# Graph attention on one core: the fold of a chunk in spaced steps, and TensorE as the one that frees a group of counts

## The chip, the cores and the metric

The kernel runs on one core of a Trainium2 chip. The metric is the time of one execution on the device, in microseconds (us); lower is better. Within the core, TensorE (PE) multiplies matrices, VectorE (DVE) works elementwise, ScalarE (ACT) applies functions and copies, SyncE (SP) issues the loads. PEld is TensorE's loading of weights.

## The reference

Four residual graph layers over 6250 nodes with 64 features and 200,000 edges. Each one normalises x by rows, takes the positive part, and adds a graph operation of the result to x. The first is a degree-scaled sum over edges, the last a message-passing pair. Between them stand three attention passes over the same edges (and a loop at each node): the second residual layer has two of them one behind the other (64 to 32 features, then 32 to 64), the third has one (64 to 64). Each of the three has this form:

```
h = x @ W
logit(edge) = leaky_relu(h[src] @ a_s + h[dst] @ a_d, 0.2)
e = exp(logit - max over the edges of dst)
out[dst] = sum(e * h[src]) / sum(e) + b
```

## The kernel before

The edges are first counted into a dense matrix of 6272 x 6272 counts (49 x 49 blocks of 128), which lies in DRAM. Each attention layer l (0, 1, 2) then goes through it in 7 chunks of 896 target nodes (CW, 7 blocks). A chunk has 49 tiles r, one for each block of 128 source nodes: a tile is counts of 128 sources by 896 targets in fp16. Seven tiles are a group. SP loads groups into four buffers (CS = 4), each group in two transfers (`load_group`, line 668), and waits for `cnt_free` before it overwrites a buffer.

The leaky ReLU has two slopes, so the exponential of a logit splits into a product of a source factor and a target factor on either side of zero. For each tile:

- ACT writes the sign, 0 or 1, of (source score + target score) for each pair (`signs`, line 3366), into one of 7 places (RING).
- DVE multiplies it with the counts: `above` (`count_above`, line 2000; in layer 0, one tile of seven finds its sign by itself, line 1997). Then `below` = counts - above (`count_below`, line 2010). Layer 2 has a `below` for every tile. Layer 1 has none for tiles 0 and 2 of a group (the `whole` tiles), where PE takes the counts themselves and subtracts by a third set of matmuls (line 2751). Layer 0 has one for tiles 1 and 5 of a group only. `below` of tile r stands behind `above` of tile r + 1 on DVE.
- PE multiplies the blocks of both sides with weighted features and adds into PSUM (line 2740): 7 matmuls a side. The last three tiles of a chunk (LATE) are taken bank group by bank group (line 2772), so that ACT can copy the first banks out while PE still works on the others. `tile_used` tells ACT that the place of a tile is free; so ACT is at most 7 tiles ahead of PE.

At tile 4 (EVICT_AT) of the next chunk ACT copies the banks of the last one to SBUF (`keep_banks`, lines 3381 and 3383), before it makes the sign of tile 4. From tile 8 (FOLD_AT) DVE folds them: the three bf16 pieces of a sum are added and both sides are scaled by target factors and added, in 5, 9 and 4 steps (FOLD_STEPS; `fold_pieces` in layers 0 and 2, `fold_levels` in layer 1), one step behind each tile, at tiles 8, 9, 10 and so on. In the last chunk of a layer all steps stand together at tile 8.

In layer 1 the fold's last step gives means. PE turns them (`turn_means`, before tile TURN_AT = 17, line 2789), ACT keeps them (KEEP_AT = 24, lines 3390 and 3391), PE multiplies them with the layer's weights (`mix_means`, MIX_AT = 26, line 2800) and ACT writes the chunk's sums (`means_out`, OUT_AT = 33, line 3398). In layer 1's last chunk DVE also does the residual and the variance of finished chunks, in three parts behind tiles 13, 22 and 36 (`residual_early_split`; its k is the tile less 13).

In layer 0, PE frees a group of counts with its last matmul on it. In layers 1 and 2, DVE frees it, behind `below` of the group's last tile, with a drain (line 2012).

Of the kernel before, what the change touches and what calls it, by code (L numbers as in the profile page):

```python
# [69 lines left out]
LATE = 3  # L70
FOLD_AT = 8
FOLD_STEPS = (5, 9, 4)
TURN_AT = 17
KEEP_AT = 24
MIX_AT = 26
OUT_AT = 33
WHOLE = (0, 2)
LW = 3 * (D + 1)
UNITS = 4
# [22 lines left out]
def gnn_kernel(nc, ap, out):  # L102
    ctx = ExitStack()
    with ctx:
# [420 lines left out]
        def groups_full(l):  # L525

            return len(parts[l][7]) - (l > 0)
# [485 lines left out]
        def _(dve):  # L1013
# [592 lines left out]

            def residual_early_split(k):

                for i, (first, b0, b1) in enumerate(((0, 0, 16), (9, 16, 32), (23, 32, EARLY))):
                    if k == 0 and i == 0:  # L1610
                        si_columns(2)
                    if k == first:
                        dve.wait_ge(sums_kept, (3, 5, 6)[i])
                    for q, step in enumerate((mixed_bias, residual, mean_of, centred, squared, variance)):
                        if k == first + 1 + q:
                            step(b0, b1)
                if k == 31:
                    dve.sem_inc(root_in, 1)

            def residual_early(k, n=1):  # L1620
# [262 lines left out]
            def split_attention(l, n):  # L1883
# [118 lines left out]
                def count_below(c, r):  # L2002

                    g, j = divmod(r, GRP)
                    if whole(l, r):
                        return
                    if l == 1 and j == GRP - 1:
                        dve.wait_ge(tile_used, c * NB + (n * ROWS + g * GRP + max(WHOLE) + 1))
                    dve.wait_ge(above_ready, c * NB + (n * ROWS + r + 1))
                    nc.vector.tensor_tensor(below_at[r % RING], counts_of(g, j), above_at[r % RING], ALU.subtract).then_inc(below_ready, 1)  # L2010
                    if l > 0 and j == GRP - 1:
                        dve.drain().then_inc(cnt_free, 1)  # L2012

                def fold_pieces(c, k):

# [84 lines left out]
                def chunk(c, first, last):  # L2100

                    for r in range(NB):
# [7 lines left out]
                        if last and r == FOLD_AT:  # L2110
                            for k in range(FOLD_STEPS[l]):
                                fold(c - 1, k)
                        elif not first and not last and 0 <= r - FOLD_AT < FOLD_STEPS[l]:
                            fold(c - 1, r - FOLD_AT)
                        if last and r >= EARLY_AT:
                            if l == 0:
                                hidden_early(r - EARLY_AT, True)
# [161 lines left out]
        def _(pe):  # L2279
# [361 lines left out]
            def split_attention(l, n):  # L2641
# [72 lines left out]
                def tile(c, r, first):  # L2714
# [5 lines left out]
                    for side in range(2):  # L2720
# [13 lines left out]
                        for b in range(CB):  # L2734
# [6 lines left out]
                                                    start=(r == 0 and at == 0), stop=False, skip_group_check=True)  # L2741
                            if l == 0 and side == 1 and b == (CB - 1 if with_below(l, r) else 0):
                                last.then_inc(tile_used, 1)
                            if l == 0 and side == 1 and b == CB - 1 and j == GRP - 1:
                                last.then_inc(cnt_free, 1)
                    if whole(l, r):
                        if first and r == 0:
# [8 lines left out]
                def late_tiles(c):  # L2756

                    for k in range(len(groups)):
                        for r in range(NB - LATE, NB):
# [8 lines left out]
                            for i, (side, b) in enumerate(members):  # L2768
                                of = above_at[r % RING] if side == 0 else below_at[r % RING] if lower else counts_of(g, j)
                                bank, at = places[side][b]  # L2770
                                wide = wide3 if l == 0 and lower else moves[side].shape[2]
                                last = nc.tensor.matmul(psum[:, bank, at:at + wide], of[:, b * BLK:(b + 1) * BLK], moves[side][:, r, 0:wide],  # L2772
                                                        start=False, stop=(r == NB - 1), skip_group_check=True)
                                if k == len(groups) - 1 and i == (len(members) - 1 if lower else 0):
                                    last.then_inc(tile_used, 1)
                            if r == NB - 1 and k < groups_full(l):
                                last.then_inc(banks_full, 1)
                    if l == 0:
# [695 lines left out]
```

## Time and profile before

| what | value |
|---|---|
| median of 3 runs | 2841.45 us (2840.66 to 2842.64) |
| the profiled execution | 2841.15 us |
| its span (first to last instruction) | 2838.9 us |
| PE busy | 2431.0 us (86%) |
| DVE busy | 2203.5 us (78%) |
| ACT busy | 1548.5 us (55%) |
| the attention layers with what lies between them | 1034 to 2335 us |
| mean granted clock of TensorE | 0.942 |

Busy shares are means over stages with different limits; the attention layers are read chunk by chunk. The granted clock is a share of full speed: 1.00 is 2.4 GHz and 0.50 is 1.2 GHz. The durations of DVE's and ACT's instructions overlap in the records: a tile operation of DVE is recorded with 0.62 us, but the next one starts 0.535 us after it; a sign on ACT is recorded with 1.04 us and the next starts 0.935 us after it. So costs are taken from start to start.

### The profile page before, as it was taken

The page shows a single profiled execution, that of the slowest core. Times are in us where ns is not written, and L with a number is a line of the kernel's source. Part 1 is how long each engine was busy: PE and PEld are TensorE (multiplying, and loading weights), DVE is VectorE, ACT ScalarE, POOL GpSimd, SP SyncE. Part 2 cuts the span into 40 slices and gives each one's busy share as a digit, 9 for nine tenths or more (in the row PEclk, how much of TensorE's full clock was granted, in tenths as well). Part 3 has the DMA queues.
Part 4 walks back from the last instruction along what each step waited for, and adds up shares of the span by engine and source line. Part 5 has one row for each costly group of instructions (what it writes and reads, how often), then busy time and mean ns, then how long its engine had stood idle before and what let it go on. Part 6 is the DMA issues. An engine that isn't in the chain of part 4 may idle for free. (4 is left out here: it accounts for less than half of the span.)

```text
span 2838.9 us, 86445 instructions
## 1 busy us (share of the span) xinstructions
PE 2431.0 (86%) x31023; PEld 2188.3 (77%) x31024; DVE 2203.5 (78%) x4979; ACT 1548.5 (55%) x1943; POOL 424.0 (15%) x921
## 2 busy tenths in 40 slices
PE   2656999999999679999599998769999868999998
PEld 2644777677777569988599888669999858898997
DVE  8986899898899879999799899799999984222212
ACT  6004444444444289998799987588888740000101
POOL 1003555555556300000000000000000000000000
PEclk8877999999999889999899999989999979999999
DMA  3003443533435347676356655225655437888998
GB/s 107 0 0 87 127 127 88 166 87 108 145 87 149 99 160 266 234 265 215 104 189 205 226 181 181 91 92 183 204 181 181 158 115 247 308 306 299 330 366 299
DMA packets 398046, 494.28 MB, mean 174 GB/s; under 512 B 81925, under 2 KB 397289, under 8 KB 397674
## 3 DMA queue, kind: packets, MB, share of 16 engines
q1 hardware_dynamic: 364760, 487.44, 51.0%
q10 hardware_dynamic: 33044, 3.63, 1.0%
q8 instruction: 150, 2.46, 0.4%
q14 instruction: 92, 0.75, 0.1%
HBM read 401.81 MB, written 89.17 MB: 173 GB/s over the span
## 5 line engine op out<-in xcount | busy, mean ns | idle before, releaser
L2740 PE MATMUL psum<-sb_arena 128*128 128x99 bf16 (+2 forms) x13524 | 1011.3, 236 | 127.7 <-DVE sb_arena L2010 82.6
L2740 PEld LDWEIGHTS psum<-sb_arena 128*128 128x128 f16 x13524 | 969.7, 99 | 157.2 <-DVE sb_arena L2010 103.0
L3366 ACT ACTIVATE sb_arena<-sb_arena 128x896 f16 (+1 forms) x980 | 961.7, 1036 | 152.4 <-PE psum L2740 107.4
L2000 DVE TENSOR_TENSOR sb_arena<-sb_arena 128x896 f16<-128x896 f16 x980 | 593.0, 621 | 84.9 <-ACT sb_arena L3366 55.2
L3035 ACT ACTIVATE sb_arena<-psum 128x784 f16<-128x784 f32 x392 | 322.5, 823 | 394.6 <-PE psum L2385 226.5
L1280 DVE TENSOR_SCALAR sb_arena<-sb_arena 128x392 f16<-128x392 f16 x1960 | 486.9, 323 | 0.0
L2385 PE MATMUL psum<-sb_arena 64*128 64x392 f16 x3920 | 387.0, 341 | 70.1 <-ACT sb_arena L3035 25.0
L2835 PE MATMUL psum<-sb_arena 128*128 128x192 bf16 x4802 | 416.2, 248 | 30.4 <-DVEq L2157 15.2
L2835 PEld LDWEIGHTS psum<-sb_arena 128*128 128x128 f16 x4802 | 402.5, 98 | 46.0 <-DVEq L2157 16.1
L2010 DVE TENSOR_TENSOR sb_arena<-sb_arena 128x896 f16<-128x896 f16 x686 | 424.0, 618 | 0.3
L2385 PEld LDWEIGHTS psum<-sb_arena 64*128 64x128 bf16 x3920 | 258.3, 138 | 151.3 <-issue 79.8
L940 POOL TENSOR_TENSOR sb_arena<-sb_arena 128x15 f32<-128x15 f32 x392 | 252.4, 644 | 271.0 <-DVE sb_arena L1280 144.3
L2368 PE MATMUL psum<-sb_arena 128*128 128x195 bf16 x2940 | 286.8, 250 | 1.6 <-ACT sb_arena L3008 1.6
L2368 PEld LDWEIGHTS psum<-sb_arena 128*128 128x128 f16 x2940 | 241.6, 98 | 57.0 <-issue 54.1
L1277 DVE TENSOR_TENSOR sb_arena<-sb_arena 128x1280 bf16<-128x1280 bf16 x196 | 162.0, 827 | 76.3 <-PE psum L2385 56.5
L2310 PE MATMUL psum<-sb_arena 128*64 128x98 bf16 x1568 | 98.4, 228 | 61.5 <-DVE sb_arena L1140 61.3
L2310 PEld LDWEIGHTS psum<-sb_arena 128*64 128x64 bf16 x1568 | 90.0, 125 | 70.0 <-DVE sb_arena L1140 70.0
L1140 DVE TENSOR_TENSOR sb_arena<-sb_arena 128x2744 bf16<-128x2744 bf16 x112 | 141.1, 1334 | 3.2 <-PE psum L2310 2.0
L942 POOL CAST sb_arena<-sb_arena 128x5 bf16<-128x5 f32 x392 | 126.2, 322 | 0.0
L2255 DVE SCALAR_TENSOR_TENSOR sb_arena<-psum,sb_arena 128x256 f32<-128x256 f32 (+1 forms) x42 | 14.5, 386 | 141.9 <-PE psum L2835 140.8
L3442 ACT COPY sb_arena<-psum 128x896 f32<-128x896 f32 x7 | 6.3, 907 | 199.2 <-PE psum L2849 199.2
L3447 ACT ACTIVATE sb_arena<-sb_arena 128x448 f32<-128x448 f32 x7 | 4.0, 577 | 183.6 <-DVEq L2265 183.6
(381 smaller groups left out, 1444.5 us busy)
## 6 DMA issues: line engine op xcount, KB each, us to landing
sb_arena<-counts SPq DMA_DIRECT2D x245, 896.0 KB, 6.9
sb_arena<-counts SPq DMA_DIRECT2D x245, 672.0 KB, 4.6
counts<-sb_arena SPq DMA_DIRECT2D x56, 1344.0 KB, 6.7
sb_arena<-records SPq DMA_DIRECT2D x392, 5.0 KB, 2.1
sb_arena<-records ACTq DMA_DIRECT2D x392, 5.0 KB, 2.2
counts<-sb_arena SPq DMA_DIRECT2D x1, 5488.0 KB, 19.8
records<-sb_arena SPq DMA_DIRECT2D x1, 3124.0 KB, 8.9
counts<-sb_arena SPq DMA_DIRECT2D x14, 112.0 KB, 4.6
```

The source lines that it names most:

```text
L940: nc.gpsimd.tensor_tensor(rel[:, k % WH, :].rearrange("p (t c) -> p t c", c=3), both[:, :, 0:3], of.broadcast_to([BLK, ST, 3]), ALU.add)
L1277: nc.vector.tensor_tensor(sub_src[:, at // 2], iota_t[:, :, 0:2 * ST], src_rel[:, k:k + 2, :].rearrange("p w t -> p (w t)").unsqueeze(1).b ...
L1280: last = nc.vector.tensor_scalar(sub_key[:, at, t, :], sub_iota[:], rel[:, k, 3 * t:3 * t + 1], None, ALU.is_equal)
L2000: nc.vector.tensor_tensor(above_at[r % RING], above_at[r % RING], counts_of(g, j), ALU.mult).then_inc(above_ready, 1)
L2010: nc.vector.tensor_tensor(below_at[r % RING], counts_of(g, j), above_at[r % RING], ALU.subtract).then_inc(below_ready, 1)
L2310: last = nc.tensor.matmul(psum[0:M, 0, 0:W], hot_row[:, s, t // 2, :, t % 2], hot_col[:, s, t // 2, :, t % 2], start=False, stop=False, sk ...
L2368: last = nc.tensor.matmul(psum[p0:p0 + d1 - d0, 6 + u // 2, u % 2 * LW:(u % 2 + 1) * LW], stage[:, slot, r * HALF + d0:r * HALF + d1], LM[ ...
L2385: last = nc.tensor.matmul(banks_of(odd, k)[:, side, 0:NB * SUB], sub_src[rows, s // 2, :, k % 2 * ST + t], sub_key[rows, s, t, :], start=t ...
L2740: last = nc.tensor.matmul(psum[:, bank, at:at + wide], of[:, b * BLK:(b + 1) * BLK], moves[side][:, r, 0:wide], start=(r == 0 and at == 0) ...
L2835: last = nc.tensor.matmul(psum[:, bank + b % 4, at:at + 3 * D], counts_of(g, j)[:, b * BLK:(b + 1) * BLK], of[:, r, :], start=(r == 0 and ...
L3035: nc.scalar.activation(to[:, :, k // EG, :, k % EG, :].rearrange("p a k d -> p k a d"), banks_of(odd, k)[:, :, 0:NB * SUB].rearrange("p k ...
L3366: nc.scalar.activation(above_at[r % RING], of, ACT.Sigmoid, bias=steep_s[:, r:r + 1], scale=STEEP).then_inc(signs_ready, 1)
```

## The change

The steps of a middle chunk's fold stand 4, 2 and 8 tiles apart (FOLD_EVERY): layer 0 at tiles 8, 12, 16, 20, 24; layer 1 at 8, 10 and so on to 24; layer 2 at 8, 16, 24, 32. What stands behind the means in layer 1 moves back: turning from tile 17 to 27, keeping from 24 to 32, mixing from 26 to 34, the sums from 33 to 39. The third part of the residual in layer 1's last chunk starts at k = 28 instead of 23, and the root's signal comes at k = 35 instead of 31. In layers 1 and 2, a matmul of PE (the second block of the lower side of the group's last tile) frees the group of counts; DVE's drain with that signal is gone. DVE's wait for `tile_used` in layer 1 stays.

```diff
 FOLD_STEPS = (5, 9, 4)
-TURN_AT = 17
-KEEP_AT = 24
-MIX_AT = 26
-OUT_AT = 33
+FOLD_EVERY = (4, 2, 8)
+TURN_AT = 27
+KEEP_AT = 32
+MIX_AT = 34
+OUT_AT = 39
...
-                for i, (first, b0, b1) in enumerate(((0, 0, 16), (9, 16, 32), (23, 32, EARLY))):
+                for i, (first, b0, b1) in enumerate(((0, 0, 16), (9, 16, 32), (28, 32, EARLY))):
...
-                if k == 31:
+                if k == 35:
                     dve.sem_inc(root_in, 1)
...
                     nc.vector.tensor_tensor(below_at[r % RING], counts_of(g, j), above_at[r % RING], ALU.subtract).then_inc(below_ready, 1)
-                    if l > 0 and j == GRP - 1:
-                        dve.drain().then_inc(cnt_free, 1)
...
-                        elif not first and not last and 0 <= r - FOLD_AT < FOLD_STEPS[l]:
-                            fold(c - 1, r - FOLD_AT)
+                        elif not first and not last and r >= FOLD_AT and (r - FOLD_AT) % FOLD_EVERY[l] == 0 and (r - FOLD_AT) // FOLD_EVERY[l] < FOLD_STEPS[l]:
+                            fold(c - 1, (r - FOLD_AT) // FOLD_EVERY[l])
...
-                            if l == 0 and side == 1 and b == CB - 1 and j == GRP - 1:
+                            if side == 1 and b == (CB - 1 if l == 0 else 1) and j == GRP - 1:
                                 last.then_inc(cnt_free, 1)
...
                                     last.then_inc(tile_used, 1)
+                                if l > 0 and r == NB - 1 and (side, b) == (1, 1):
+                                    last.then_inc(cnt_free, 1)
```

## Rows read from the trace of the kernel before

**Rows 1.** Stretches (us): length, busy of PE, PEld, DVE, ACT, POOL, granted clock, DMA.

```profile
1168.00:1212.80 44.80, 41.80 (x687) 40.92 (x688) 41.48 (x69) 41.96 (x48) 0.00 (x0) 1.00 0.73 251
1400.80:1451.60 50.80, 50.80 (x784) 50.60 (x785) 48.56 (x88) 49.59 (x55) 0.00 (x0) 0.96 0.50 164
1563.50:1619.70 56.20, 52.70 (x796) 50.86 (x794) 51.49 (x102) 50.44 (x58) 0.00 (x0) 0.97 0.59 200
1571.50:1586.00 14.50, 11.00 (x141) 9.44 (x138) 12.77 (x31) 10.29 (x12) 0.00 (x0) 0.88 0.48 163
2050.70:2111.80 61.10, 58.64 (x689) 57.95 (x687) 57.21 (x104) 52.45 (x54) 0.00 (x0) 1.00 0.56 187
```

**Rows 2.** Waits from 1034 to 2335 us: total, times, longest.

```profile
PE psum L2740 <- DVE sb_arena L2010: 82.6, 72, 5.7
```

**Rows 3.** Timeline of DVE in layer 2, chunk 3: start, length, instructions, idle before.

```profile
2052.57 0.62 DVE L2000 TENSOR_TENSOR sb_arena<-sb_arena 128x896 f16<-128x896 f16 x1 [1.78 <-ACT sb_arena L3366]
...
2055.80 0.62 DVE L2000 TENSOR_TENSOR sb_arena<-sb_arena 128x896 f16<-128x896 f16 x1
...
2057.16 0.63 DVE L2000 TENSOR_TENSOR sb_arena<-sb_arena 128x896 f16<-128x896 f16 x1 [0.22 <-issue]
...
2066.11 0.63 DVE L2000 TENSOR_TENSOR sb_arena<-sb_arena 128x896 f16<-128x896 f16 x1 [0.19 <-issue]
...
2107.77 0.62 DVE L2010 TENSOR_TENSOR sb_arena<-sb_arena 128x896 f16<-128x896 f16 x1
```

**Rows 4.** Timeline of PE in the same chunk of layer 2.

```profile
2063.05 1.35 PE L2740 MATMUL psum<-sb_arena 128*128 128x195 bf16 x14 [0.90 <-DVE sb_arena L2010]
...
2067.33 7.88 PE L2740 MATMUL psum<-sb_arena 128*128 128x195 bf16 x91 [0.53 <-DVE sb_arena L2010]
...
2108.27 3.72 PE L2772 MATMUL psum<-sb_arena 128*128 128x195 bf16 x42
```

**Rows 5.** Timeline of DVE in layer 0, chunk 3.

```profile
1172.47 0.62 DVE L2000 TENSOR_TENSOR sb_arena<-sb_arena 128x896 f16<-128x896 f16 x1 [0.16 <-ACT sb_arena L3366]
...
1180.27 0.63 DVE L2000 TENSOR_TENSOR sb_arena<-sb_arena 128x896 f16<-128x896 f16 x1 [0.19 <-issue]
...
1191.50 0.62 DVE L2010 TENSOR_TENSOR sb_arena<-sb_arena 128x896 f16<-128x896 f16 x1
```

**Rows 6.** Timeline of PE in the same chunk of layer 0.

```profile
1181.49 15.75 PE L2740 MATMUL psum<-sb_arena 128*128 128x99 bf16 x262 [1.18 <-DVE sb_arena L2010]
```

**Rows 7.** Timeline of DVE in layer 1, chunk 3.

```profile
1569.73 0.63 DVE L2000 TENSOR_TENSOR sb_arena<-sb_arena 128x896 f16<-128x896 f16 x1 [0.21 <-issue]
...
1585.55 1.16 DVE L2000 TENSOR_TENSOR sb_arena<-sb_arena 128x896 f16<-128x896 f16 x2 [0.21 <-issue]
...
1595.50 0.61 DVE L2010 TENSOR_TENSOR sb_arena<-sb_arena 128x896 f16<-128x896 f16 x1
```

**Rows 8.** Timeline of PE in the same chunk of layer 1.

```profile
1586.66 0.67 PE L2789 MATMUL psum<-sb_ident,sb_arena 128*128 128x128 f32 x4
...
1596.01 1.01 PE L2800 MATMUL psum<-sb_W_att,sb_arena 128*128 128x264 f32 x4
1596.86 2.90 PE L2740 MATMUL psum<-sb_arena 128*128 128x198 bf16 x42
```

**Rows 9.** Timeline of ACT in the same chunk of layer 1.

```profile
1561.96 0.80 ACT L3383 COPY sb_arena<-psum 128x792 f32<-128x792 f32 x1
...
1564.06 12.24 ACT L3366 ACTIVATE sb_arena<-sb_arena 128x896 f16 x13
...
1597.30 0.51 ACT L3398 COPY sb_arena<-psum 128x448 f32 x1
1598.05 1.98 ACT L3366 ACTIVATE sb_arena<-sb_arena 128x896 f16 x2 [0.24 <-PE psum L2740]
```

**Rows 10.** Issues of DMAs: KB each, median us from issue to landing.

```profile
sb_arena<-counts SPq DMA_DIRECT2D x245, 896.0 KB, 6.9
```

**Rows 11.** Timeline of PE at the end of layer 1's last chunk.

```profile
1806.06 2.78 PE L2772 MATMUL psum<-sb_arena 128*128 128x198 bf16 x38 [0.56 <-DVE sb_arena L2010]
```

## The prediction

> **What bounds the kernel now.** I first read the stretches of the span chunk by chunk, taking one middle chunk of each attention layer [rows 1]. A middle chunk lasts 44.8 us in layer 0, 56.2 in layer 1 and 61.1 in layer 2. In each of them TensorE (PE), VectorE (DVE) and ScalarE (ACT) are all busy for over 85% of the time, so no single engine is the bound: the chain through the ring of seven tiles is. The list of waits shows where the loss appears: PE waits for `below` tiles of DVE 72 times, 82.6 us [rows 2].
>
> The timelines of one chunk then show who is late where. In what follows a chunk starts with PE's first matmul, at 1168.03, 1563.45 and 2050.71 us in the three layers. In layer 2, DVE has no free time after tile 4. It waits 1.78 us for the sign of tile 4, since ACT has just copied the banks, and after that it runs back to back to the next chunk [rows 3]. PE stands still only in the fold, at tiles 9 to 11: 0.90, two later waits of which the last is 0.53, then nothing [rows 4]. So a chunk is two chains joined at one tile: DVE from the sign of tile 4 to the tile where PE catches up, and PE from there to the end. The chunk's length is the largest value, over the tiles r, of "end of r's tiles on DVE, plus what PE has left from r". An edit pays only as far as it lowers this for every r.
>
> **What the change removes.** *The drain behind each group's last `below`* (layers 1 and 2, seven a chunk). Three tiles without it take 3.23 us on DVE (start of tile 4 at 2052.57 to start of tile 7 at 2055.80), 1.08 each; from tile 7 to tile 8, with it between, it is 1.36 (2055.80 to 2057.16) [rows 3]. So 0.29 us each, counting the exact 1.07 of two operations at 0.535. Its signal moves to a matmul that PE issues anyway; layer 0 has that form already, at no cost that I can see in its rows. Zero is the other bound for the drain, if DVE would have waited there anyway. The Trainium skill speaks for that zero (VectorE: DVE Perf Modes, Rules for kernel authors): a drain follows each DVE operation whatever one does, so count operations, not semaphores. By it the removal is worth nothing; the trace shows 0.29 us start to start for exactly this place, and I keep the row.
>
> *The fold's steps apart.* Their number and work stay the same. In layer 0, DVE goes from tile 8 at 1172.47 to tile 13 at 1180.27 [rows 5], 7.80 us; less five tile operations at 0.535 and the one of 1.07 (3.75), so 4.05 us of fold. In layer 1, tile 8 to 17 is 1569.73 to 1585.55 [rows 7], 15.82 us; 15 operations and one drain are 8.33, so the fold is 7.5. In layer 2, tile 8 to 12 is 2057.16 to 2066.11 [rows 3], 8.95 less 4 x 1.07 = 4.7. All this stays on DVE; spread, it only comes due later.
>
> **Layer 2, five middle chunks.** With steps at 8, 16, 24 and 32 and no drains, PE's stop at 9 to 11 goes. What ties next is the last tile: PE's late tiles begin at 2108.27 and touch tile 48 after eight matmuls of 0.085 us, at 2108.95 [rows 4]; DVE ends `below` of tile 48 at 2107.77 + 0.62 = 2108.39 [rows 3]. That is 0.56 us of slack, 0.50 after 0.06 for the signal, which is how far PE's starts stay behind DVE's ends in the fold. Six drains lie before it, 1.77 us. So the chunk shrinks by 2.27 to 58.8. PE's own floor is 686 matmuls x 0.0848 = 58.2. Tile 24, where three steps are done, gives 58.4 by the same sum, so tile 48 decides. I take 2.3 us x 5 = 11.5 us.
>
> **Layer 0, five middle chunks.** No drain is removed. All five steps are done by tile 24, so DVE ends `below` of tile 26 exactly as before: 1191.50 + 0.62 = 1192.12 [rows 5]. PE comes to it 196 matmuls after 1181.49 at 0.0594 us each, 1193.13 (15.5 us over 262 matmuls) [rows 6]: 1.0 us of slack, 0.95 with the signal. That is all the gain; before tile 26 the spread steps leave shorter sums (tile 22: 43.4 us). The chunk becomes 43.9; 0.9 x 5 = 4.5 us.
>
> **Layer 1, five middle chunks.** The steps end at tile 24, and turning the means (0.50 us on PE, 1586.66 to 1587.16) and mixing them (0.85, 1596.01 to 1596.86) [rows 8] now both come after tile 26 instead of before it. DVE ends `below` of tile 26 at 1595.50 + 0.61 = 1596.11 [rows 7], less three drains 1595.2. PE started the second side of tile 26 at 1596.86 + 7 x 0.085 = 1597.46, and needed 22.2 us to the chunk's end at 1619.7; now 22.2 + 0.50 + 0.85 = 23.6. Sum: 1595.2 + 0.06 - 1563.45 + 23.6 = 55.4 us. Second, ACT: `means_out` now stands 5 tiles behind the mixing, not 7, and the ring lets ACT be 7 ahead of PE, so ACT waits for the mixing at tile 39. PE is at tile 26's second side at 1595.27; the rest of it is 0.31 us, five plain tiles are 0.91 each (three take 2.74, from the row of 42 matmuls at 1596.86), two whole ones 1.21 [rows 8], 7.3 in all, so the mixing ends at 1595.27 + 7.3 + 1.35 = 1603.9; the copy costs ACT 0.75 (1597.30 to 1598.05); then sign 39 starts at 1604.7, 13 signs at 0.935 lead to sign 3 of the next chunk, and 0.935 and the bank copies (1561.96 to 1564.06, 2.10) to sign 4, at 1619.9: 55.8 after 1564.06 [rows 9]. Between 55.4 and 55.8 I take 55.6: 0.6 x 5 = 3.0 us.
>
> **The other chunks.** Chunk 0 has no fold and PE is bound in it (50.8 us, all of it PE busy, [rows 1]): nothing. The last chunks keep their fold in one piece at tile 8. In layer 1 DVE is bound to the end there (PE waits for it in the late tiles, [rows 11]), six drains at 0.25 (my estimate, a little under the 0.29 above, since some waiting is mixed in) give 1.5 us; the third part of the residual moves five tiles back but is the same work, and its wait for the sums is met by `means_out` at tile 39 against tile 41. In layer 2, DVE is bound up to tile 36: five drains, 1.3 us. After the layers nothing changes.
>
> **The loads.** PE frees a group of counts up to 3 us later than DVE did, in SP's queue. Tightest is group 2 of the next chunk: freed in the late tiles, about 1 us before the chunk starts, needed by DVE at tile 14, some 14 us into it. The larger half of a load lands 6.9 us after issue in the median [rows 10]; with group 3 queued beside it I bound it by twice that, 13.8. So even at that bound the 15 us cover it, by 1 us; a wait there would cost its own length once a chunk.
>
> **Sum.** 11.5 + 4.5 + 3.0 + 1.5 + 1.3 = 21.8 us. The profiled execution took 2841.15 us, 0.3 below the median of the three runs, so 2819.4 profiled and 2819.6 for the median.
>
> **The rivals.**
> *The forecast*, 2812 to 2827: 0.62.
> *Layer 1 gives nothing*, since the waits of ACT at tiles 32 and 39 eat it: 2822.6 to 2826. For it: DVE tile 48 of layer 1 would have only some 0.3 us left. 0.12.
> *All of PE's stops go*: PE busy is 41.8, 50.8 and 58.2 us a chunk, so 3.0 + 5.4 + 2.9 = 11.3, x 5 and 2.8: 2782. Against it: DVE's own work from tile 4 on, which spreading doesn't shorten. 0.07.
> *The drain is worth nothing*: then layer 2 gives 0.5 x 5, layer 0 4.5, layer 1 nothing: 7 us, 2834.4. This is the skill's rule above; the 0.29 us row speaks against it. 0.06.
> *Slower, by TensorE's clock.* Layer 1's fold stretch ran at a mean granted clock of 0.88, so partly at 1.2 GHz, after PE had idled in it; the chunk as a whole has 0.97 [rows 1]. After the change PE has many short waits over tiles 8 to 26 in place of a few long ones. If the low level held for that stretch, a layer-1 tile would cost PE about twice 0.91 us against DVE's 1.25 or so with the fold: 0.57 over 18 tiles is some 10 us a chunk, 50 in the layer: 2870. It decides from about 4 us a chunk on. Against it: the chunks of layers 0 and 2 ran at 1.00 all through, though PE idled some 2.5 us of the 6 from tile 9 to 12 in layer 2 [rows 1, 4]. The Trainium skill (TensorE: Matmul & The Clock Gate, Part 1) says that the throttled state is the default and activity lifts it; the trace agrees in layer 1 only, and sharper idling is what the change takes away. 0.06.
> *Late loads*: 2 to 3 us of waiting in each of ten chunks, 2840 to 2850; only if a load took over 15 us. 0.03. *No change*, from causes that I don't see: 0.04.
>
> **How the numbers follow.** 0.2% (5.7 us) is about what a measurement of this kernel tells from no change. Faster is the sum of the first four, 0.87; slower the clock and most of the late loads, 0.08; same 0.05. The range leaves out the clock, the full recovery and part of the drain's case: 2806 (layer 0 at its floor, layer 1 by its first sum, layer 2 at 58.2) to 2830.
>
> **What would show it.** Right: no drain row at the old place; middle chunks of 43.9, 55.6 and 58.8 us; PE's wait in one piece gone, short ones at tiles 12 to 26 in layers 0 and 1, and one at the late tiles of layer 2; ACT idle at tile 39 in layer 1. Wrong: DVE start to start still 1.36 across a group's end, DVE waiting for counts, or a clock under 1.00 in layers 0 and 2.

## The result, and the profile after

| | before | after |
|---|---|---|
| median | 2841.33 us (4 runs, 2840.66 to 2842.64) | 2821.56 us (4 runs, 2821.03 to 2825.98) |
| profiled execution | 2841.15 us, span 2838.9 us | 2821.03 us, span 2818.8 us |
| mean granted clock | 0.942 | 0.946 |

The ratio is 0.9933, with a 95% interval of 0.9921 to 0.9945: faster by 19.8 us, where 21.8 were forecast. In the kernel after, the line numbers differ from those of before by one: `above` is L2001, `below` L2011, the signs L3367, PE's tiles L2739 and its late tiles L2771.

The list of waits between 1034 and 2335 us, of the kernel after, in the columns of [rows 2]:

```profile
PE psum L2739 <- DVE sb_arena L2011: 64.7, 76, 5.5
...
DVE sb_arena L2001 <- ACT sb_arena L3367: 54.9, 67, 4.3
DVE sb_arena L2001 <- issue: 4.4, 25, 0.2
```

PE's wait for `below` fell from 82.6 us to 64.7 [rows 2], though it happens more often: 76 times and not 72. The third line is what a removed drain looks like in a list of waits: before, `above` started after an empty moment of 0.2 us 75 times, 14.2 us in all. DVE has no wait for a load of counts among its waits, so the loads are on time.

One middle chunk of each layer (chunk 3), and the last chunk of layer 1, in the columns of [rows 1]:

```profile
1167.06:1210.90 43.84, 41.91 (x686) 40.95 (x686) 41.15 (x69) 42.03 (x48) 0.00 (x0) 1.00 0.75 256
1560.20:1615.90 55.70, 52.59 (x797) 49.36 (x794) 51.07 (x101) 49.96 (x59) 0.00 (x0) 1.00 0.59 202
2041.00:2099.90 58.90, 58.57 (x690) 58.09 (x688) 56.67 (x104) 52.67 (x54) 0.00 (x0) 1.00 0.56 191
1727.40:1804.50 77.10, 59.97 (x795) 55.81 (x792) 68.39 (x122) 47.35 (x56) 0.00 (x0) 0.87 0.43 146
```

The forecast was 43.9, 55.6 and 58.8 us for the first three. PE's busy time in them is what it was; its idle time went. The clock column of layer 1 shows 1.00 where [rows 1] have 0.97.

From here on a *period* is the time from PE's first matmul of a chunk to its first of the next (for a layer's last chunk, to the start of its own last matmul). Periods in the profiled executions, in us:

| | before | after | difference x count |
|---|---|---|---|
| layer 0, middle chunks | 44.8 | 43.87 | 4.6 |
| layer 1, middle chunks | 56.24 | 55.71 | 2.7 |
| layer 1, last chunk | 76.45 | 77.11 | -0.7 |
| layer 2, middle chunks | 61.11 | 58.80 | 11.5 |
| layer 2, last chunk | 98.76 | 96.47 | 2.3 |
| layer 0's last matmul to layer 1's first | 49.18 | 50.66 | -1.5 |
| layer 1's last matmul to layer 2's first on counts | 60.44 | 59.69 | 0.7 |

These are 19.6 of the 20.1 us between the two profiled executions (with rounding); the rest lies in the chunks 0 and around the layers. The chunk's number counts from 0, and the middle chunks are 1 to 5.

**Layer 2 after.** DVE, chunk 3 (its first PE matmul at 2041.04 us), in the columns of [rows 3]:

```profile
2042.90 0.63 DVE L2001 TENSOR_TENSOR sb_arena<-sb_arena 128x896 f16<-128x896 f16 x1 [1.59 <-ACT sb_arena L3367]
...
2046.12 0.62 DVE L2001 TENSOR_TENSOR sb_arena<-sb_arena 128x896 f16<-128x896 f16 x1
...
2047.19 0.62 DVE L2001 TENSOR_TENSOR sb_arena<-sb_arena 128x896 f16<-128x896 f16 x1
...
2067.92 1.17 DVE L2031 TENSOR_TENSOR sb_arena<-sb_arena 128x455 f32<-128x455 f32 x2
2069.23 0.63 DVE L2001 TENSOR_TENSOR sb_arena<-sb_arena 128x896 f16<-128x896 f16 x1
2069.78 0.62 DVE L2011 TENSOR_TENSOR sb_arena<-sb_arena 128x896 f16<-128x896 f16 x1
...
2096.30 0.61 DVE L2011 TENSOR_TENSOR sb_arena<-sb_arena 128x896 f16<-128x896 f16 x1
```

PE in the same chunk, with the columns of [rows 4]:

```profile
2041.04 29.23 PE L2739 MATMUL psum<-sb_arena 128*128 128x195 bf16 x343
2070.45 25.69 PE L2739 MATMUL psum<-sb_arena 128*128 128x195 bf16 x301 [0.18 <-DVE sb_arena L2011]
2095.97 0.84 PE L2771 MATMUL psum<-sb_arena 128*128 128x195 bf16 x8
2096.97 3.05 PE L2771 MATMUL psum<-sb_arena 128*128 128x195 bf16 x34 [0.15 <-DVE sb_arena L2011]
```

Tiles 7 and 8 now start 1.07 us apart across the group's end (2046.12 to 2047.19), not 1.36 [rows 3]. PE's stop at tiles 9 to 11 [rows 4] is gone. Two short stops are left, and both stand where `below` ends 0.05 or 0.06 us before PE goes on: at the fold's third step (2069.78 + 0.62 = 2070.40, PE at 2070.45) and in the late tiles, after eight matmuls (2096.30 + 0.61 = 2096.91, PE at 2096.97). The second is the tie at tile 48 of which the forecast was made.

**Layers 0 and 1 after.** In layer 0 the last short stop of PE is at tile 26, then 273 matmuls run through; the `below` that it waits for is the second line (DVE), ending at 1191.23:

```profile
1191.29 16.42 PE L2739 MATMUL psum<-sb_arena 128*128 128x99 bf16 x273 [0.22 <-DVE sb_arena L2011]
...
1190.61 0.62 DVE L2011 TENSOR_TENSOR sb_arena<-sb_arena 128x896 f16<-128x896 f16 x1
```

In layer 1 PE has short stops from tile 8 to 26 (0.15 to 1.23 us). ACT waits twice: 1.52 us for the turned means at tile 32, and 0.97 us for the mixing before it copies the sums at tile 39. The last three lines are ACT's, in the columns of [rows 9]:

```profile
1575.23 2.46 PE L2739 MATMUL psum<-sb_arena 128*128 128x99 bf16 x35 [1.23 <-DVE sb_arena L2011]
...
1600.15 1.01 PE L2801 MATMUL psum<-sb_W_att,sb_arena 128*128 128x264 f32 x4
...
1593.36 0.27 ACT L3391 COPY sb_arena<-psum 128x128 f32<-128x128 f32 x1 [1.52 <-PE psum L2790]
...
1601.29 0.53 ACT L3399 COPY sb_arena<-psum 128x448 f32 x1 [0.97 <-PE psum L2801]
1601.72 13.17 ACT L3367 ACTIVATE sb_arena<-sb_arena 128x896 f16 x14
```

### The profile page after: what moved, and what is told of

The parts are those of the page before. It is cut to its first block and busy times, and to the rows that moved or that the text cites. A ratio compares the mean times of both kernels' runs of the same rounds, so it can differ in the third digit from the quotient of the medians.

```text
span 2818.8 us, 86346 instructions
## 1 busy us (share of the span) xinstructions
PE 2428.7 (86%) x31023; PEld 2181.7 (77%) x31024; DVE 2194.9 (78%) x4979; ACT 1547.7 (55%) x1943; POOL 425.1 (15%) x921
## 5 line engine op out<-in xcount | busy, mean ns | idle before, releaser
L2739 PE MATMUL psum<-sb_arena 128*128 128x99 bf16 (+2 forms) x13524 | 1009.5, 235 | 104.3 <-DVE sb_arena L2011 64.7
L2739 PEld LDWEIGHTS psum<-sb_arena 128*128 128x128 f16 x13524 | 963.2, 99 | 138.3 <-DVE sb_arena L2011 89.6
L3367 ACT ACTIVATE sb_arena<-sb_arena 128x896 f16 (+1 forms) x980 | 960.0, 1038 | 112.5 <-PE psum L2739 71.1
L2001 DVE TENSOR_TENSOR sb_arena<-sb_arena 128x896 f16<-128x896 f16 x980 | 592.1, 620 | 71.8 <-ACT sb_arena L3367 54.9
L2011 DVE TENSOR_TENSOR sb_arena<-sb_arena 128x896 f16<-128x896 f16 x686 | 423.4, 617 | 0.5
## 6 DMA issues: line engine op xcount, KB each, us to landing
counts<-sb_arena SPq DMA_DIRECT2D x1, 5488.0 KB, 19.8
```

The lines of the kernel that those rows point to most:

```text
L2001: nc.vector.tensor_tensor(above_at[r % RING], above_at[r % RING], counts_of(g, j), ALU.mult).then_inc(above_ready, 1)
L3367: nc.scalar.activation(above_at[r % RING], of, ACT.Sigmoid, bias=steep_s[:, r:r + 1], scale=STEEP).then_inc(signs_ready, 1)
```

## The experiments

**The theory.** A chunk's period is the largest value over the tiles r of "end of r's tiles on DVE, plus what PE has left from r". It follows that the drains and the spacing are worth little alone and much together in layer 2, and that the tile that decides can be moved by moving steps. *Rivals:* the two edits simply add; the drain costs nothing; the clock does it.

All runs are against the kernel before on the same chip. The totals scatter by some us from run to run, but the periods of undisturbed middle chunks with the same code agree within about 0.1 us from profile to profile, so the verdicts go by periods, each from one profiled execution (chunk 1 of each layer differs, in layer 1 by up to 0.8 us, and is left out; layer 2's last chunk scatters by up to 0.9 us, 96.47 and 95.61 for the same kernel). Periods in us:

| kernel | layer 0 | layer 1 | layer 2 | layer 1 last | layer 2 last | median us, ratio [95%] |
|---|---|---|---|---|---|---|
| drains alone | 44.8 | 55.72, once 56.27 | 60.81 | 75.07 | 96.59 | 2831.51, 0.9973 [0.9964, 0.9983] |
| spacing alone | 43.87 | 56.55 | 60.62 | 77.85 | 98.54 | 2836.88, 0.999 [0.998, 0.9999] |
| means wider | 43.88 | 55.49 | 58.82 | 76.28 | 96.65 | 2819.72, 0.9924 [0.9907, 0.994] |
| layer 1 in one piece | 43.9 | 55.72, once 56.05 | 58.81 | 75.07 | 96.46 | 2820.63, 0.9931 [0.9914, 0.9947] |
| residual earlier | 43.88 | 55.72 | 58.81 | 75.36 | 96.62 | 2821.13, 0.9925 [0.9901, 0.9949] |
| steps 8, 2, 2 apart | 43.3 | 55.72 | 60.45 | 77.10 | 96.14 | 2827.72, 0.9951 [0.9937, 0.9965] |
| layer 1 turned at 25 | 43.88 | 55.15 | 58.81 | 76.86 | 96.79 | 2821.4, 0.9931 [0.9906, 0.9956] |
| two late tiles in layer 2 | 43.87 | 55.71 | 58.73 | 77.11 | 95.90 | 2821.29, 0.9929 [0.9906, 0.9952] |
| three edits together | 43.3 | 55.16 | 58.82 | 76.67 | 95.53 | 2816.27, 0.9914 [0.99, 0.9928] |
| the changed kernel again | 43.87 | 55.71 | 58.82 | 77.13 | 95.61 | 2822.14, 0.9928 [0.9914, 0.9942] |
| layer 1 as before | 43.88 | 56.24 | 58.82 | 76.46 | 96.75 | 2823.31, 0.9935 [0.9917, 0.9953] |
| the kernel before again | 44.8 | 56.24, once 56.63 | 61.12, once 62.05 | 76.44 | 98.99 | 2839.82, a single run |

The values marked "once" are of a chunk with a stretch at half clock (granted clock 0.50; see runs 11 and 12).

What a run saves in its middle chunks need not show in its total. Runs 5, 7 and 8 have medians of 2821.13 to 2821.4 us, as the kernel after has (2821.56). In run 7's profile, against that of the kernel after, the middle chunks of layer 1 save 2.8 us, while 1.2 us are lost between layers 1 and 2 and 1.9 behind the attention layers, where the code is the same. So these runs show what a chunk costs, and not a faster kernel.

**1. Drains alone.** The kernel before, without the drain:

```diff
-                    if l > 0 and j == GRP - 1:
-                        dve.drain().then_inc(cnt_free, 1)
...
-                            if l == 0 and side == 1 and b == CB - 1 and j == GRP - 1:
+                            if side == 1 and b == (CB - 1 if l == 0 else 1) and j == GRP - 1:
                                 last.then_inc(cnt_free, 1)
```

> Only the drains are gone and PE frees the counts; fold, means and residual stand as in the kernel before. Theory (a chunk is DVE's chain up to the tile where PE catches up, then PE's): a drain pays only if it lies before that tile. Layer 0 44.8 us a middle chunk, layer 1 55.6 (two drains before tiles 15 to 20), layer 2 60.8 (one before tiles 9 to 11), total 2833 to 2835. Rival (gains of the two parts just add, a drain is worth 0.29 us wherever it stands): 54.2 and 59.0 us in layers 1 and 2, total about 2818 to 2822. Rival (a drain costs nothing): 56.2, 61.1, total 2841.

Layer 2 came as the theory has it (60.81), layer 1 0.1 us above (55.72). The total, 2831.5, lies 1.5 us below the expected range; the last chunks of layers 1 and 2 gave 1.4 and 2.2 us.

**2. Spacing alone.** The changed kernel with the drain put back, so that steps, means and residual stand as changed:

```diff
+                    if l > 0 and j == GRP - 1:
+                        dve.drain().then_inc(cnt_free, 1)
```

> The fold's steps, the means and the residual's third part stand as in the changed kernel, but DVE frees the counts behind a drain as before. Theory: layer 0 43.9 us a middle chunk, layer 1 56.3 to 56.4 (both the turning and the mixing are now behind tile 26, no gain), layer 2 60.6 (six drains again before tile 48), total 2835 to 2838. Rival (PE's stop in the fold is the loss, and the spacing alone removes it): layer 1 about 55.5, layer 2 58.8, total near 2822.

Layers 0 and 2 and the total came as expected; layer 1 took 56.55, 0.15 us more than the theory has.

In layer 2 the drains alone give 0.30 us a chunk, the spacing alone 0.49, and both 2.31. PE's stops in chunk 3 say why. Drains alone (PE, the chunk from 2044.6 us on):

```profile
2056.64 1.35 PE L2738 MATMUL psum<-sb_arena 128*128 128x195 bf16 x14 [0.59 <-DVE sb_arena L2010]
2059.03 1.36 PE L2738 MATMUL psum<-sb_arena 128*128 128x195 bf16 x14 [1.04 <-DVE sb_arena L2010]
2060.93 41.10 PE L2738 MATMUL psum<-sb_arena 128*128 128x195 bf16 x483 [0.53 <-DVE sb_arena L2010]
```

Spacing alone (PE, the chunk from 2048.5 us on):

```profile
2068.60 9.66 PE L2741 MATMUL psum<-sb_arena 128*128 128x195 bf16 x112 [0.39 <-DVE sb_arena L2011]
2078.80 25.89 PE L2741 MATMUL psum<-sb_arena 128*128 128x195 bf16 x301 [0.54 <-DVE sb_arena L2011]
...
2106.23 3.05 PE L2773 MATMUL psum<-sb_arena 128*128 128x195 bf16 x34 [0.56 <-DVE sb_arena L2011]
```

Without the drains the fold in one piece still stops PE three times at tiles 9 to 11; one drain lies before that place, and 0.30 is one drain. With the spacing PE meets DVE at the last tile instead, and the six drains before that tile are the bound. By the medians they give 9.5 us and 4.2 (before: 2841.04 in these runs) where both together give 19.8; by the ratios of the table it is 7.7 and 2.8 against 19.0. Either way the edits don't add.

**3. Means wider apart.** The keeping, mixing and sums of layer 1 later:

```diff
-KEEP_AT = 32
-MIX_AT = 34
-OUT_AT = 39
+KEEP_AT = 34
+MIX_AT = 36
+OUT_AT = 43
```

> The changed kernel with the ACT steps of layer 1 seven tiles behind PE's again (keeping at 34, mixing at 36, sums at 43). Theory that ACT's waits at tiles 32 and 39 hold the chunk: layer 1 falls from 55.7 to 55.4 or 55.5 us a middle chunk, PE's first tile no longer waits for the bank copies, and the total gains 1 to 1.5 us. Rival (the chain DVE to tile 26, then PE, holds it, ACT's waits are covered): 55.7 us, no change. Layers 0 and 2 as in the changed kernel, 43.9 and 58.8.

Layer 1's middle chunks took 55.49, not 55.71, and ACT's waits for turned and mixed means are both gone (ACT; chunk 3 from 1558.2 us on):

```profile
1593.37 8.04 ACT L3367 ACTIVATE sb_arena<-sb_arena 128x896 f16 x8 [0.18 <-PE psum L2750]
1601.32 0.51 ACT L3399 COPY sb_arena<-psum 128x448 f32 x1
```

So ACT's waits were what held layer 1, by 0.22 us, and behind them stands the other sum of the prediction (55.4). The edit takes both away at once; in the kernel after it is the later one, for the mixing, that reaches the chunk's end, since ACT runs through its 14 signs from there to the next bank copies.

**4. Layer 1's fold in one piece**, on the changed kernel, with the means and the residual's third part where they were before:

```diff
-FOLD_EVERY = (4, 2, 8)
-TURN_AT = 27
-KEEP_AT = 32
-MIX_AT = 34
-OUT_AT = 39
+FOLD_EVERY = (4, 1, 8)
+TURN_AT = 17
+KEEP_AT = 24
+MIX_AT = 26
+OUT_AT = 33
```

> The changed kernel with layer 1 as before the change but for the drains: its nine steps at tiles 8 to 16, means at 17, 24, 26 and 33, the residual's third part at k = 23. Theory: layer 1 55.6 us a middle chunk, so the spacing gives layer 1 nothing beyond the drains; its last chunk falls from 77.1 to about 75, since PE no longer stands idle just before the late tiles, and the total is 2818 to 2820. Rival (spacing is what gained in layer 1): 56.2 us a chunk and 2824. Layers 0 and 2 at 43.9 and 58.8.

The middle chunks took 55.72 as in the changed kernel: spacing the fold in layer 1 is worth nothing as such. The last chunk took 75.07, as expected, and the total 2820.63.

**5. The residual's third part earlier:**

```diff
-... enumerate(((0, 0, 16), (9, 16, 32), (28, 32, EARLY))):
+... enumerate(((0, 0, 16), (9, 16, 32), (25, 32, EARLY))):
```

> The changed kernel with the residual's third part of layer 1's last chunk three tiles earlier (k = 25, tiles 38 to 44). The work is the same. Theory: in the changed kernel it ends one tile before the late tiles, PE waits on DVE there, its clock falls, and the late matmuls run at 1.2 GHz; earlier, PE's late tiles run at 2.4 GHz and the last chunk of layer 1 falls from 77.1 to about 75.3 us, by some 1.8, all else equal (layers 0, 1, 2: 43.9, 55.7, 58.8 a middle chunk). Rival (the later place costs DVE a wait for the sums, or the clock falls there anyway): 77 us again.

Layer 1's last chunk took 75.36 us instead of 77.11. PE's last lines in that chunk, first in the kernel after, then with the residual earlier; [rows 11] are the same place before:

```profile
1797.95 0.51 PE L2771 MATMUL psum<-sb_arena 128*128 128x198 bf16 x4 [1.35 <-DVE sb_arena L2011]
1800.03 4.73 PE L2771 MATMUL psum<-sb_arena 128*128 128x198 bf16 x38 [1.57 <-DVE sb_arena L2011]
```

```profile
1800.18 0.51 PE L2771 MATMUL psum<-sb_arena 128*128 128x198 bf16 x4 [0.58 <-DVE sb_arena L2011]
1801.25 2.77 PE L2771 MATMUL psum<-sb_arena 128*128 128x198 bf16 x38 [0.56 <-DVE sb_arena L2011]
```

The same 38 matmuls take 4.73 us in the one and 2.77 in the other (2.78 before, [rows 11]). The stretches around them show the granted clock (the value behind POOL's), of the kernel after and of this one:

```profile
1797.90:1804.80 6.90, 5.25 (x42) 4.51 (x42) 2.46 (x5) 2.13 (x4) 0.00 (x0) 0.56 0.00 1
```

```profile
1800.10:1804.00 3.90, 3.24 (x42) 2.66 (x42) 1.63 (x4) 1.60 (x4) 0.00 (x0) 1.00 0.01 2
```

In the kernel after, the residual's third part ends at tile 47. PE idles for 1.35 and 1.57 us in the late tiles, and their matmuls run mostly at 1.2 GHz. The waits themselves cost nothing: DVE ends `below` of tile 48 73.14 us into the chunk in the kernel after and 73.27 in this one. The whole difference of 1.75 us comes behind that point, in the 38 matmuls.

**6. Steps 8, 2 and 2 apart**, to move the deciding tile of layers 0 and 2:

```diff
-FOLD_EVERY = (4, 2, 8)
+FOLD_EVERY = (8, 2, 2)
```

> The changed kernel with other distances: layer 0 at 8, 16, 24, 32, 40, layer 2 at 8, 10, 12, 14. Theory (the largest sum over the tiles decides): in layer 0 the tie at tile 26 goes, the next one is the late tiles (slack 0.75 us, less 0.06), so 43.2 us a middle chunk; in layer 2 all the fold is done by tile 14, where 0.06 us of slack and two drains (0.59) are all there is, so 60.4 to 60.5. Layer 1 at 55.7. Rival (only taking the steps apart matters, not where the last one stands): 43.9 and 58.8.

Layer 0 takes 43.3 and layer 2 60.45, close to the theory (43.2, and 60.4 to 60.5). Layer 0's last chunk took 1.4 us more (50.59), though its code is unchanged; see runs 9 and 10.

**7. Layer 1's steps at 8, 10, 12, 14, 16, 18, 20, 22, 23**, turn at 25, sums at 41.

```diff
-FOLD_EVERY = (4, 2, 8)
-TURN_AT = 27
+FOLD_TILES = ((8, 12, 16, 20, 24), (8, 10, 12, 14, 16, 18, 20, 22, 23), (8, 16, 24, 32))
+TURN_AT = 25
...
-OUT_AT = 39
+OUT_AT = 41
```

> The changed kernel with layer 1's last fold step at tile 23 instead of 24, the means turned before tile 25 instead of 27, and the sums written at 41 instead of 39. Theory: PE's 0.50 us of turning is no longer behind tile 26, and ACT keeps seven tiles from PE at both steps, so layer 1 falls from 55.7 to 55.1 or 55.2 us a middle chunk, total 2.5 us less. Rival (tile 26 is not what ties): 55.5, as with the wide means alone. Layers 0 and 2 at 43.9 and 58.8.

55.15, as the theory has it. Of the 0.56 us, 0.22 are what the wider means alone gave (run 3); the other 0.34 come with the turn of 0.50 us standing in front of tile 26, where PE would wait. The 2.5 us in the total did not come (2821.4).

**8. Two late tiles in layer 2:**

```diff
+                late = 2 if l == 2 else LATE
...
-                        for r in range(NB - LATE, NB):
+                        for r in range(NB - late, NB):
...
-                    for r in range(NB - LATE):
+                    for r in range(NB - late):
```

> The changed kernel with two late tiles instead of three in layer 2. Theory that PE's need for tile 48 at the start of the late tiles alone holds layer 2: PE needs it 0.84 us later, the chunk falls from 58.8 to PE's floor of 58.2. Rival: ACT's bank copies (1.0 us each) no longer fit behind the late matmuls of a group (0.68 instead of 1.02), sign 4 and with it DVE's tile 4 come about 0.9 us later after PE's first tile, and what is won at tile 48 is lost there: 58.8 or a little more, with a wait of PE for the bank copies at its tile 0. I expect the rival.

58.73, 0.08 less than 58.81. The late tiles are no longer where PE waits (2037.98 on, one row of 28 matmuls), but DVE gets its sign of tile 4 later, 2.10 us after PE's start (2040.35 to 2042.45) and not 1.86 (2041.04 to 2042.90), and PE now stops at tile 24 alone (the last line):

```profile
2037.98 2.53 PE L2773 MATMUL psum<-sb_arena 128*128 128x195 bf16 x28
2040.35 7.82 PE L2739 MATMUL psum<-sb_arena 128*128 128x195 bf16 x88
...
2042.45 0.63 DVE L2001 TENSOR_TENSOR sb_arena<-sb_arena 128x896 f16<-128x896 f16 x1 [1.51 <-ACT sb_arena L3369]
...
2070.00 26.88 PE L2739 MATMUL psum<-sb_arena 128*128 128x195 bf16 x315 [0.22 <-DVE sb_arena L2011]
```

From the chunk's start to that stop's end it is 29.65 us, and the 343 matmuls left at 0.0848 take 29.08: 58.73, the measured period. So the tie went from tile 48 to tile 24, whose sum the later sign had raised by 0.24. Little was won, as the rival has it, but PE's wait for the bank copies, which the rival expects at tile 0, did not come.

**9. Three edits together**: layer 0's steps 8 apart, layer 1's as in run 7, the residual's third part as in run 5, with the sums at 39 in the last chunk:

```diff
-FOLD_EVERY = (4, 2, 8)
+FOLD_TILES = ((8, 16, 24, 32, 40), (8, 10, 12, 14, 16, 18, 20, 22, 23), (8, 16, 24, 32))
...
```

> The changed kernel with three edits together: layer 0's fold steps at tiles 8, 16, 24, 32, 40; layer 1's at 8, 10, 12, 14, 16, 18, 20, 22, 23 with the turn of the means at 25 and means_out at 41 (at 39 in the last chunk); the residual's third part three tiles earlier. If a chunk is the largest of its sums over the tiles and the edits touch different layers, they add: layer 0's middle chunks 43.3 us (0.57 less, x 5 = 2.9), layer 1's 55.15 (0.56 less, x 5 = 2.8), layer 1's last chunk about 75.3 (1.8 less), layer 2's middle chunks 58.8 as they are: 7.5 us less than the changed kernel, about 2813.7 in all, a ratio near 0.990. The rival, that the clock takes back between and around the chunks what the chunks save (a stretch at the low level falling on layer 0's or layer 1's last chunk, as with steps 8 apart, where layer 0's last chunk took 50.6 instead of 49.2): 2815 to 2819, with the middle chunks as forecast and the loss in the last chunks or the gap between the layers. Wrong altogether: middle chunks of 43.9 and 55.7.

**10. The changed kernel again**, on the same chip.

> The changed kernel as it is, beside the combination on the same chip, so that the two can be compared at five rounds each. Expected: 2821.6 us as before, within 1.5; the same chunk periods (43.87, 55.7, 58.8) and, if the stretch at the low clock in layer 1's last chunk is a fixed consequence of the order of the work, a last chunk of 77.1 again with the clock at 0.50 from about 1799 us on; if it is chance from run to run, 75.4 and a dip elsewhere.

2816.27 us against 2822.14: 5.9 us less by the medians, though the two ratios' intervals (0.99 to 0.9928, and 0.9914 to 0.9942) still overlap. The middle chunks came as forecast (43.3, 55.16, 58.82), and those of layers 0 and 1 make 5.2 us of it, all ten summed. The last chunk of layer 1 doesn't follow: 76.67, not 75.3. PE's late matmuls there, with the wait lines alike to run 5's:

```profile
1791.26 0.51 PE L2771 MATMUL psum<-sb_arena 128*128 128x198 bf16 x4 [0.58 <-DVE sb_arena L2011]
1792.34 4.37 PE L2771 MATMUL psum<-sb_arena 128*128 128x198 bf16 x38 [0.56 <-DVE sb_arena L2011]
```

The waits are the same (0.58, 0.56), the 38 matmuls take 4.37 and not 2.77: here the stretch at half clock begins 73.4 us into the chunk and covers them, in run 5 it begins at 77.5, after them. So what made the step "1.5 us in layer 1's last chunk" fail is the low clock over the late tiles, but avoiding PE's idle time right before them isn't enough to be rid of it. In all seven profiles with the residual's third part at its new place (the kernel after and runs 2, 3, 6, 7, 8 and 10) a stretch at 0.50 lay over the late tiles; of the seven with it three or five tiles earlier, only run 9 has one. So the place matters, and it doesn't decide alone. The changed kernel repeated its own picture (77.13, half clock from 71.2 us on, against 71.3).

Run 6's loss in layer 0 is of the same kind. PE in the last chunk of layer 0, first in run 6, then in run 9, which has the same code there:

```profile
1302.18 7.62 PE L2739 MATMUL psum<-sb_arena 128*128 128x99 bf16 x98 [2.79 <-DVE sb_arena L2011]
...
1316.66 8.52 PE L2739 MATMUL psum<-sb_arena 128*128 128x99 bf16 x112 [1.34 <-DVE sb_arena L2011]
```

```profile
1303.75 7.62 PE L2739 MATMUL psum<-sb_arena 128*128 128x99 bf16 x98 [2.77 <-DVE sb_arena L2011]
...
1318.23 6.99 PE L2739 MATMUL psum<-sb_arena 128*128 128x99 bf16 x110 [1.35 <-DVE sb_arena L2011]
```

The waits ahead agree within 0.02 us, yet 112 matmuls took 8.52 us in the one and 110 took 6.99 in the other (the code is the same, so two records are missing there). Run 6 has a second stretch of 3.41 us at 0.50, from 1316.7; run 9 has its second one only at 1346.0, between the layers, where it costs 1.5 us as in the kernel after.

**11. The kernel before again, and 12. layer 1 as before.** The second is run 4 with layer 1's drains put back, so that layer 1 is that of the kernel before and layers 0 and 2 are changed:

```diff
+                    if l == 1 and j == GRP - 1:
+                        dve.drain().then_inc(cnt_free, 1)
```

After run 1 a doubt was left: every middle chunk of layer 1 before had a stretch at half clock. The 0.5 us there could be the clock's and not the drains'.

> The kernel before, once more with a profile. All its middle chunks of layer 1 (56.24 us) had a stretch at half clock of 3.41 us. With drains alone gone the chunks with such a stretch took 56.27 and those without 55.72, so what layer 1 gained may be the clock and not the drains. If the drains are worth nothing there, any middle chunk without a stretch at the low clock takes 55.7; if they are worth what the prediction gives them, it takes 56.2 or so, like the others. If every middle chunk has its stretch again (layer 0's chunks last the same, so the phase may repeat), this run tells only that the stretches come from the order of the work and are no chance: 56.24 five times.

> The changed kernel with layer 1 as before altogether: its fold in one piece, turn at 17, keep at 24, mix at 26, sums at 33, the residual's third part at 23, and the seven drains a chunk back in layer 1 alone. Layers 0 and 2 keep the change. It differs from layer 1's steps together (55.72 without a stretch at the low clock, 56.05 to 56.55 with one) in the drains of layer 1 alone. If the drains are worth nothing there: the same 55.72 without and 56.3 with such a stretch, and a last chunk of 75.1. If they cost what the order of the work lets through (three of them before tile 26, 0.9 less what waiting hides): 56.2 to 56.5 without one, and a last chunk of 76.4 as before. The whole: 2841.3 less layer 0's 4.6, layer 2's 11.7 and 2.3, and the gap, which was 1.5 longer in all kernels with layer 0's steps four apart: 2824, or 2821 if the drains are worth nothing.

The kernel before again, chunks 2 and 3 of layer 1 (the granted clock is the value behind POOL's):

```profile
1506.10:1562.40 56.30, 51.47 (x797) 49.79 (x794) 51.47 (x101) 50.50 (x58) 0.00 (x0) 1.00 0.58 198
1562.40:1619.00 56.60, 53.86 (x796) 52.25 (x794) 51.61 (x102) 50.33 (x58) 0.00 (x0) 0.94 0.58 200
```

And drains alone, chunks 3 and 4:

```profile
1561.30:1617.00 55.70, 52.46 (x796) 50.84 (x793) 51.18 (x101) 50.45 (x58) 0.00 (x0) 0.97 0.59 202
1617.00:1673.30 56.30, 53.66 (x797) 52.28 (x795) 51.36 (x101) 50.38 (x58) 0.00 (x0) 0.94 0.59 200
```

With the drains a chunk takes 56.24 us at a mean clock of 0.97 ([rows 1], and all of run 12's) and 56.27 at 1.00 (the first line). Without them it takes 55.72 at 0.97 (the third line) and at 1.00. So the 0.52 us are the drains', whatever the clock; one stretch of 3.41 us costs nothing in these chunks (run 4 has one in which it cost 0.33). (The expectation took run 1's larger period for one of a short stretch; it belongs to one of 6.83 us.) The longer stretch, of 6.83 us, costs 0.4 us with the drains and 0.55 without, the second and fourth line, at 0.94. Run 12 took 76.46 us in layer 1's last chunk, against 75.07 in run 4, so the drains cost 1.4 us there. It came to 2823.31 us in all, where 2824 was forecast for drains that cost.

## Why the prediction was right, and where not

*Layer 2, 11.5 us: right, and for its reason.* 2.31 x 5 = 11.5, with the tie at tile 48 and the sum of tile 24 some 0.3 us below it (58.5, where the prediction has 58.4): PE's eight matmuls from 2095.97 on end at 2096.65 by 0.085 each, and it goes on at 2096.97. Runs 1 and 2 exclude that the edits just add (0.30 + 0.49), run 6 that any spacing does it.

*The drain's price, 0.29 us: right.* The distance of the tiles across a group's end fell by 0.29. The rival that took it for nothing read that out of the Trainium skill (VectorE: DVE Perf Modes, Rules for kernel authors), which says of chained operations that the drain happens regardless and that their count matters, not the semaphores. For the drain that this kernel adds itself the rival is refuted: taking these away alone gives 9.5 us by the medians and 7.7 by the ratio (run 1). Where DVE isn't the bound they are free: of layer 2's seven, six gave nothing as long as the fold stood in one piece (0.30 us a chunk, run 1).

*Layer 0, 4.5 us: right.* 0.93 x 5 = 4.6, and PE's last stop is the one for `below` of tile 26, 0.06 us behind it.

*Layer 1, 3.0 us: right within 0.3.* Of the two sums, ACT's (55.8) and DVE's (55.4), ACT's was the bound at 55.71, and with ACT's waits taken away 55.49 came, close to the other. That ACT's sum hit within 0.1 us is in part luck: the mixing began 39.9 us into the chunk (1600.15 - 1560.23), where the prediction has 39.6, and the copy of the sums cost ACT 0.43 us (1601.29 to 1601.72), where it has 0.75. The gain comes from the drains (0.52 a chunk, runs 1, 4, 11 and 12), not from the spacing: with the drains still in, the spaced form is the slower one (56.55, run 2), and without them both take 55.72. The prediction hadn't split it.

*Layer 1's last chunk, 1.5 us: this step failed.* It reads "six drains at 0.25 give 1.5 us; the third part of the residual moves five tiles back but is the same work". DVE did end earlier, by 1.22 us: `below` of tile 48 ends 73.14 us into the chunk (before 74.36). The six drains are worth about what it says: 1.4 us, in run 1 against before and in run 12 against run 4. But with the residual at its new place the clock was low over PE's late tiles, the last 38 matmuls took 4.73 us and not 2.78, and the chunk ended 4.0 us after DVE and not 2.1. So -0.7 for +1.5. "The same work" was true of DVE; what its place would do to PE's clock was put at nothing. Why the stretch falls there stays open, since run 9 has it with the shorter waits too.

*Layer 2's last chunk, 1.3 us: the mechanism right, the size too small.* 2.3 us, of which the drains alone gave 2.2 (98.76 to 96.59): as much as all seven at 0.31, where five were taken. This chunk scatters by up to 0.9 us, so the count isn't settled to one drain.

*Between the layers, 0: off by -1.5 and +0.7.* A stretch at half clock of 3.41 us began in the matmuls between layers 0 and 1 (at 1351.6 us in the kernel after, at 1346.0 to 1353.2 in the others), in the kernels with a changed layer 0 except run 6 (50.4 to 50.7 us between the layers), and not in the kernels whose layer 0 is that of before (49.1 to 49.3). What triggers it there isn't settled.

*The rival "slower, by TensorE's clock"* didn't come in the middle chunks: with stops of 0.15 to 1.23 us spread over tiles 8 to 26, layer 1 ran at a granted clock of 1.00 in all five. It did appear in small, in layer 1's last chunk and between the layers, some 3.4 us in all. *Late loads* didn't appear. In sum 21.8 was forecast and 19.8 measured; the two errors of the last chunks (-2.2, +1.0) and the gap between the layers make up the difference.

## What to carry to other kernels

Where two engines meet through a ring, write the period as the largest value over the tiles of "producer's end of this tile plus consumer's rest". An edit pays until the next tile ties, and two edits that are worth 0.30 and 0.49 us alone can be worth 2.31 together; so when one alone brings nothing, look at which tile decides before dropping it. How far apart a side job's steps stand matters, since those done by a tile count in its sum: layer 0 took 43.3 us with steps 8 apart and 43.87 with 4, layer 2 took 60.45 with steps 2 apart and 58.81 with 8. Put what the consumer does on its own (the turn of the means) where it would wait anyway. And look at what stands just before a burst of matmuls at a stage's end: here the longer waits there cost nothing by themselves, but the low clock that came with them cost 2 us.

## What was not expected of the hardware

The same matmuls behind the same waits ran at different clocks in different kernels: 38 late matmuls took 2.77 us or 4.37 us behind waits of 0.58 and 0.56 us each time, and 110 or so took 6.99 or 8.52 us. So the waits just before don't decide alone whether the granted clock falls to 0.50. Run 9's last chunk of layer 0, which lacks the second stretch, began 1.6 us later than run 6's (1293.77 and 1292.18 us); that such a shift is what brings or removes a stretch is not shown.

What such a stretch costs hangs on PE's slack where it falls: 3.41 us at 1.2 GHz cost nothing in most of layer 1's middle chunks, 0.33 us in one (56.05 against 55.72, run 4), 0.93 us in a middle chunk of layer 2 (62.05 against 61.12, run 11) and 1.5 us among the matmuls between layers 0 and 1.
